# Attention and expert kernel: projections of local units an iteration earlier, parts stored once and repeated by the loads

## Chip, core and metric

One NeuronCore of a Trainium2 chip. The metric is the device time of one execution in microseconds (us); lower is better. Times come from repeated runs and from one profiled execution, whose trace has every instruction of the engines: PE (TensorE), DVE (VectorE), ACT (ScalarE), POOL (GpSimd) and SP (SyncE, which here only issues transfers).

## What is computed

Two layers on x of shape 8 x 512 x 128. Layer 1: attention with 16 heads of size 8 in which a query sees itself and 128 keys before it, an output projection, residual, layer norm. Layer 2: layer norm, causal attention with 16 heads, projection, residual, then a top-2 mixture of 8 experts (128 to 512 to 128, gelu), residual and layer norm. Cut to the attention:

```python
scores = jnp.einsum('bhtd,bhsd->bhts', q, k) * scale
scores = jnp.where(allowed, scores, -jnp.inf)   # j <= i, and j >= i - 128 in layer 1
attn = jax.nn.softmax(scores, axis=-1)
out = jnp.einsum('bhts,bhsd->bhtd', attn, v)
```

## The kernel before

**Units and iterations.** A unit is one batch element in one layer: units 0 to 7 are local (layer 1), 8 to 15 causal (layer 2). The iterations run from -2 to 16; iteration `it` does the scores, exponents, masks and values of unit `it`, the row maxima of unit `it + 1` (and the first of `it + 2`), and the tail (division, output projection, norms, routing) of unit `it - 1`. An iteration has 14 steps if its layer is local, 20 if causal (6 in iteration -2); in a step TensorE fills one pair of PSUM banks with scores, one or two with products for the maxima, and multiplies older probabilities by v. The PSUM pairs form a ring of three (L182 on) that scores, maxima, projections and turned outputs share. Every engine walks the same steps in its own program order; tables fix the order: `JOBS` (L166) gives side jobs their step, `project_at` (L174) the projection of q and k, `maxima_table` (L148) the maxima.

**Stacks.** To keep f32 accuracy with bf16 matmuls, q and k (after `project`, L1299) are split in three bf16 parts: HIGH by ACT (L740), the rest by DVE (L899), MIDDLE by ACT (L745), LOW by DVE (L905). A stack has 48 rows for each of two row groups (rows 0 to 47 and 64 to 111): six slots of 8 rows, and each slot holds one part of q or of k, so that one matmul over 48 rows sums the products of parts that matter. q has HIGH in slots 0 to 2, MIDDLE in 4 and 5, LOW in 3; k has HIGH in 2 to 4, MIDDLE in 1 and 5, LOW in 0. Two more rows hold the shift, the row maximum of each query (rows 48, 49). Three pairs of stacks exist; unit u uses pair u mod 3. The rows change partition on the way, so SP stores the parts to DRAM (`parts_dram`) and loads them back (`load_stacks`, L426 to L455): per unit six stores, in which each part is written once for every slot that it fills, and ten loads of 24, 16 or 8 rows of 8 KB. There is one copy of `parts_dram`, so a unit waits for the loads of the unit before.

**Order on SP's queue.** In iteration `it`: `load_stacks(it + 2)`, x_t of unit `it + 3` if that is local (L419), x_tok (L424), in causal iterations a slice of expert weights, and at last `load_shift(it + 1)` (L460), which waits for the shift of the next unit. SP's waits hold back all behind them.

**Other lines.** L1223/L1232 and L1252/L1258 are the products for the maxima, local and causal, L867 to L881 the maxima themselves, L889/L891 the splitting of the shift, L1341 its transpose, L784 its copy. L1198 are the scores, L707 their exponents, L603 to L619 the masks, L1278 the values. Of the tail: L913/L917 division, L1328/L1334 turned and projected outputs, L928/L935 residual sum, L941 to L945 `moments`, L954/L955 `variances`, L636/L638 `root` on POOL, L963/L974 `apply`, L1349/L768 the expert input xf, L1355/L985 logits, L777 `copy_rows`, L999 to L1009 `choose`, L1364 rank, L1020 to L1030 `place`, L628 `send`, an indirect store of 128 rows by POOL (eight per causal unit); `apply` of a unit waits until the sends of the unit before have landed. After the attention, 40 blocks of 256 rows run through the experts (L1415, L1434).

Of the kernel before, what the change touches and what calls it, by code (L numbers as in the profile page):

```python
# [70 lines left out]
STACK_LOADS = 5 * TILES_R * 16  # L71
# [76 lines left out]
def maxima_table():  # L148

    table = {}  # L150
    for u in range(UNITS):
        slots = []
        if u - 2 >= -1:
            n = steps(u - 2)
            slots += [(u - 2, k) for k in range(n - LEAD[layer(u - 2)], n)]
# [12 lines left out]
    CAUSAL: {0: ("xt",), 2: ("v",), 5: ("on",), 7: ("out",), 14: ("xf",), 15: ("shift",), 16: ("logits",), 18: ("rank",)},  # L168
# [5 lines left out]
def project_at(it, k):  # L174

    if it < 0:
        return k if it == -2 and 0 <= k < 2 else None
    return it + 2 if real(it + 2) and k == (0 if layer(it + 2) == LOCAL else 1) else None


def jobs_at(it, k):
# [6 lines left out]
    return out  # L188

# [26 lines left out]
def build(nc, x_t_in, x_in, w_in_all, pack_in, out):  # L216
    ctx = ExitStack()
    with ctx:
# [104 lines left out]
        scratch = nc.dram_tensor("parts_dram", (2, SLOTS, P, T), BF16, kind="Internal").ap()  # L323
# [23 lines left out]
        stored_high, stored_low = sem("stored_high"), sem("stored_low")  # L347
# [58 lines left out]
        def _(sp):  # L406
# [19 lines left out]
            def load_stacks(u):  # L426

                def store(part, ready):
                    sp.wait_ge(ready, u + 1)
                    for side, slots in ((0, Q_SLOTS), (1, K_SLOTS)):  # L430
                        place = scratch[side, slots[part]].rearrange("s p t -> p s t")
                        sp.dma_start(place, parts[:, part, side, :].unsqueeze(1).to_broadcast(place.shape)
                                     ).then_inc(stored_low if part else stored_high, 16)

                def load(side, first, last):
                    stack = (q_st, k_st)[side][u % STACKS]
                    by_row = scratch[side].rearrange("s (d r g) t -> (s d) r (g t)", d=HD, r=TILES_R)
                    for r in range(TILES_R):
                        sp.dma_start(stack[HALF * r + first:HALF * r + last, :, :].rearrange("p g t -> p (g t)"), by_row[first:last, r, :]  # L439
                                     ).then_inc(stack_in[u % STACKS], 16)  # L440

                if u:
                    sp.wait_ge(stack_in[(u - 1) % STACKS], ((u - 1) // STACKS + 1) * STACK_LOADS)
                store(0, high_ready)
                store(1, middle_ready)
                if u >= STACKS:
                    sp.wait_ge(score_filled, BEFORE[u - STACKS + 1])
                sp.wait_ge(stored_high, (u + 1) * 32)
                for side in range(2):
                    load(side, *HIGH_ROWS[side])  # L450
                store(2, low_ready)
                sp.wait_ge(stored_low, (u + 1) * 64)
                for side in range(2):
                    for rows_of_part in LOW_ROWS[side]:
                        load(side, *rows_of_part)  # L455
# [7 lines left out]
            for it in ITERATIONS:  # L463
# [3 lines left out]
                if it >= 0 and real(it + 2):  # L467
                    load_stacks(it + 2)
# [10 lines left out]
                if real(it + 1):  # L479
                    load_shift(it + 1)  # L480

# [52 lines left out]
        def _(pool):  # L534
# [49 lines left out]
            def plan_constants():  # L584

                pool.wait_ge(stored_high, UNITS * 32)
                pool.wait_ge(stored_low, UNITS * 64)
# [881 lines left out]
```

## Time and profile before

| | us |
|---|---|
| median of 3 runs (867.06 to 868.45) | 867.57 |
| profiled execution, its own time | 870.4 |
| span from its first to its last instruction | 868.6 |
| PE busy | 655.7 (75%) |
| DVE busy | 509.7 (59%) |
| ACT busy | 462.6 (53%) |
| POOL busy | 429.8 (49%) |

The profiled execution took 2.8 us more than the median of the runs; stretches and waits are read from it. The start takes it to 54.7 us, the local iterations to about 311, the causal ones to about 644, the expert blocks to 833, the last norm to the end. A row of a timeline is: start, duration, engine, line, instruction, shapes, count, and in brackets how long its engine was idle before it and what ended that. In the rows by windows the columns are named in the group's line.

### The profile page before, as it was taken

How to read it: one execution, taken by the hardware profiler on the slowest of the kernel's cores; microseconds unless marked ns; L12 is line 12 of the kernel's file. 1: busy time of each engine (PE TensorE's matmuls, PEld its weight loads, DVE VectorE, ACT ScalarE, POOL GpSimd, SP SyncE). 2: the span in 40 equal slices, each digit the busy share in tenths (PEclk: the TensorE clock that was granted, in tenths of full speed). 3: DMA queues.
4: the chain of work that ended last, by engine and by line, in shares of the span. 5: the costliest groups of instructions: out<-in, count | busy, mean ns of one | idle time of the engine just before them, and what ended most of it. 6: DMA issues, size and time to landing. Idle time of an engine off the chain costs nothing.

```text
span 868.6 us, 19900 instructions
## 1 busy us (share of the span) xinstructions
PE 655.7 (75%) x7512; PEld 393.1 (45%) x7512; DVE 509.7 (59%) x1116; ACT 462.6 (53%) x671; POOL 429.8 (49%) x649
## 2 busy tenths in 40 slices
PE   2557978978887878888788888886614999999900
PEld 0323434434443433444343444442313998898900
DVE  1644667676776888798888879882340222222236
ACT  2035655655674565766677666666502554554503
POOL 4015556556654543245464647458640454445445
PEclk8568999998997998999999999999855999999965
DMA  5635544643643637334362707101014566566464
GB/s 170 157 90 115 138 109 100 154 126 67 159 116 46 153 97 135 102 76 135 66 159 42 185 25 190 43 16 53 20 58 161 187 204 214 184 223 213 168 163 128
DMA packets 73583, 107.45 MB, mean 124 GB/s; under 512 B 8104, under 2 KB 60048, under 8 KB 70428
## 3 DMA queue, kind: packets, MB, share of 16 engines
q1 hardware_dynamic: 68892, 97.86, 42.2%
q0 software_dynamic: 4608, 8.47, 3.3%
q8 instruction: 54, 0.88, 0.5%
q14 instruction: 29, 0.24, 0.1%
HBM read 44.14 MB, written 38.90 MB: 96 GB/s over the span
## 4 chain that ended last, share of the span: by engine, by line
PE 32%; DMA 22%; DVE 17%; issue 10%; SPq 7%; POOL 6%; ACT 4%; another core or an unknown queue 0%; POOLq 0%; ACTq 0%; DVEq 0%
DMA parts_dram<-parts 9%; DMA arena<-parts_dram 7%; PE pair_ps L1415 6%; PE o_ps L1278 6%; SPq L439 4%; PE o_ps L1434 3%; PE pair_ps L1299 3%; PE pair_ps L1198 3%; POOL rows_dram L628 3%; DMA rows_dram<-rows,row_at 3%; PE misc L1434 3%; DVE row_max L878 2%; ACT probs L707 2%; DVE row_max L876 2%; PE pair_ps L1258 1%
## 5 line engine op out<-in xcount | busy, mean ns | idle before, releaser
L707 ACT ACTIVATE probs<-pair_ps 128x1024 f32<-128x1024 f32 x272 | 275.4, 1022 | 116.2 <-PE pair_ps L1198 107.5
L1278 PE MATMUL o_ps<-probs,v_aug 128*32 128x256 f32 (+3 forms) x2048 | 166.0, 421 | 9.1 <-POOL probs L616 3.5
L603 POOL TENSOR_SCALAR_AFFINE_SELECT probs<-probs 128x512 f32<-128x512 f32 x96 | 61.2, 637 | 140.4 <-ACT probs L707 139.4
L1198 PE MATMUL pair_ps<-arena 50*128 50x256 bf16 (+3 forms) x1024 | 108.2, 288 | 26.6 <-DMA arena<-shift_t 6.5
L673 POOL DMA_INDIRECT outputs_dram<-o_norm,arena x80 | 77.7, 971 | 100.5 <-DVE o_norm L1128 80.0
L867 DVE TENSOR_REDUCE row_max<-pair_ps 128x4 f32<-128x768 f32 x96 | 89.7, 953 | 46.7 <-PE pair_ps L1232 46.1
L838 ACT ACTIVATE probs<-pair_ps,arena 128x256 f32<-128x256 f32 x160 | 65.4, 471 | 76.3 <-PE pair_ps L1415 66.0
L876 DVE TENSOR_REDUCE row_max<-pair_ps 128x2 f32<-128x1024 f32 x64 | 77.2, 1219 | 15.8 <-PE pair_ps L1258 14.7
L1415 PE MATMUL pair_ps<-x_t,arena 128*128 128x256 f32 x320 | 80.8, 397 | 7.1 <-DMA arena<-pack 3.9
L1198 PEld LDWEIGHTS pair_ps<-arena 50*128 50x128 bf16 x1024 | 32.7, 95 | 108.9 <-issue 45.5
L1278 PEld LDWEIGHTS o_ps<-probs,v_aug 128*32 128x32 f32 x2048 | 48.6, 111 | 66.0 <-issue 39.5
L628 POOL DMA_INDIRECT rows_dram<-rows,row_at x64 | 63.4, 991 | 26.6 <-issue 15.7
L1223 PE MATMUL pair_ps<-window_b,ident_b 64*64 64x256 bf16 x384 | 32.1, 324 | 51.7 <-DMA arena<-parts_dram 43.1
L1415 PEld LDWEIGHTS pair_ps<-x_t,arena 128*128 128x128 f32 x320 | 59.8, 197 | 17.0 <-issue 8.9
L1252 PE MATMUL pair_ps<-first_b,eye_b 64*128 64x128 bf16 (+2 forms) x640 | 49.0, 232 | 22.7 <-ACT probs L707 8.7
L878 DVE TENSOR_REDUCE row_max<-pair_ps 128x2 f32<-128x768 f32 x64 | 60.9, 952 | 8.9 <-PE pair_ps L1258 8.9
L1124 DVE TENSOR_TENSOR o_norm<-o_ps,arena 128x256 f32<-128x256 f32 x20 | 8.5, 425 | 97.6 <-PE o_ps L1434 75.3
L1258 PE MATMUL pair_ps<-arena 48*128 48x384 bf16 (+3 forms) x512 | 62.4, 302 | 0.0
L605 POOL TENSOR_SCALAR_AFFINE_SELECT probs<-probs 128x512 f32<-128x512 f32 x96 | 60.9, 634 | 0.0
L611 POOL TENSOR_SCALAR_AFFINE_SELECT probs<-probs 128x256 f32<-128x256 f32 x64 | 26.0, 407 | 58.2 <-ACT probs L707 57.9
L899 DVE TENSOR_TENSOR rest<-pair_ps,parts 128x1024 f32<-128x1024 f32 x16 | 19.6, 1225 | 52.0 <-ACT parts L740 52.0
L1252 PEld LDWEIGHTS pair_ps<-first_b,eye_b 64*128 64x128 bf16 x640 | 26.3, 96 | 44.9 <-ACT probs L707 18.8
(147 smaller groups left out, 1107.8 us busy)
## 6 DMA issues: line engine op xcount, KB each, us to landing
arena<-pack SPq DMA_DIRECT2D x40, 578.0 KB
arena<-parts_dram SPq DMA_DIRECT2D x96, 192.0 KB
parts_dram<-parts SPq DMA_DIRECT2D x32, 384.0 KB
parts_dram<-parts SPq DMA_DIRECT2D x32, 256.0 KB
arena<-rows_dram SPq DMA_DIRECT2D x40, 130.0 KB
pack<-in_pack SPq DMA_DIRECT2D x8, 578.0 KB, 7.4
parts_dram<-parts SPq DMA_DIRECT2D x32, 128.0 KB
arena<-parts_dram SPq DMA_DIRECT2D x32, 128.0 KB
```

The costliest lines, as they stand in the source:

```text
L628: nc.gpsimd.indirect_dma_start(out=table[:, :], out_offset=bass.IndirectOffsetOnAxis(ap=row_at[:, j:j + 1], axis=0), in_=rows[:, j // NT, ...
L673: nc.gpsimd.indirect_dma_start(out=outputs[:, :], out_offset=bass.IndirectOffsetOnAxis(ap=place, axis=0), in_=block_y[i][:, t, :], in_offs ...
L707: nc.scalar.activation(probs[:, n % PROBS, :], pair_ps[RING_AT["score", n][0]][:, :, :].rearrange("p b t -> p (b t)"), ACT.Exp, scale=SCAL ...
L838: nc.scalar.activation(hidden[:, i * FT + f, :], hidden_ps[2 * i + f // 2][:, f % 2 * BLK:(f % 2 + 1) * BLK], ACT.Gelu_apprx_tanh, bias=bl ...
L867: nc.vector.tensor_reduce(top[:, i, :, 2 * g:2 * g + 2], pair[:, :, 0:2 * WIN].rearrange("p b (s k) -> p b s k", k=WIN), AX_X, ALU.max).th ...
L876: nc.vector.tensor_reduce(top[:, 3, :, 2 * g + m], pair[:, :, :], AX_X, ALU.max).then_inc(max_done, 1)
L878: nc.vector.tensor_reduce(top[:, 2, :, 2 * g + m - 2], pair[:, :, 0:3 * P], AX_X, ALU.max)
L1198: last = nc.tensor.matmul(pair[:, r, col:col + width], k_st[u % STACKS][own, gs, j * P:(j + 1) * P], q_st[u % STACKS][own, gs, q0:q0 + wid ...
L1252: nc.tensor.matmul(target[:, :, keys], eye_b[own, HALF * (1 - half):HALF * (1 - half) + P], first_b[r][own, half, keys].unsqueeze(1).to_br ...
L1258: last = nc.tensor.matmul(pair[:, r, col:col + keys], qs[own, gs, i * P:(i + 1) * P], ks[own, gs, 0:keys], start=False, stop=(n == len(wor ...
L1278: last = nc.tensor.matmul(o_ps[c * VHEAD:(c + 1) * VHEAD, q0:q0 + width], v_aug[u % 2][:, j, first:first + VHEAD], probs[:, slot, r * T + ...
L1415: last = nc.tensor.matmul(hidden_ps[2 * i + f // 2][:, f % 2 * BLK:(f % 2 + 1) * BLK], block_w[w][:, PACK_W1 + f * P:PACK_W1 + (f + 1) * P ...
```

## The change

- `project_at`: a local unit is projected three iterations ahead, at step 8, instead of two ahead at step 0. Causal units stay at step 1, two ahead. So unit 2 is projected in iteration -1, and iteration 5 has no projection.
- Each part is stored once (three stores per unit), into one of two copies of `parts_dram`; the loads repeat it, with a source whose outermost step is zero, into the slots (14 loads per unit). A unit waits for the stacks of the unit two before, not one. `load_stacks` of a local unit comes at the end of SP's iteration, after `load_shift`.
- `maxima_table`: the maxima of unit 1 all lie in iteration 0, so none stands before the first shift on PE.
- Causal side jobs: xf at step 13 (14), rank at 19 (18), moments 8 (9), variances 9 (10), apply 11 (12), copies of rows 13 (16), sends in steps 2 to 9 (0 to 7), `root` ahead of its step's mask, `top_two` ahead of its step's maxima. What follows a job of an iteration's last step is done in the next iteration's step 0. The moves of moments, variances and apply hold for local units too.

```diff
-Q_SLOTS = (slice(0, 3), slice(4, 6), slice(3, 4))
-K_SLOTS = (slice(2, 5), slice(1, 6, 4), slice(0, 1))
-HIGH_ROWS = ((0, 24), (16, 40))
-LOW_ROWS = (((24, 48),), ((0, 16), (40, 48)))
+LOW, MIDDLE, HIGH = 0, 1, 2
+Q_PARTS = {HIGH: ((0, HIGH, 3),), MIDDLE: ((4, MIDDLE, 2),), LOW: ((3, LOW, 1),)}
+K_PARTS = {HIGH: ((2, HIGH, 3),), MIDDLE: ((1, MIDDLE, 1), (5, MIDDLE, 1)), LOW: ((0, LOW, 1),)}
...
-STACK_LOADS = 5 * TILES_R * 16
+STACK_LOADS = 7 * TILES_R * 16
...
-        if u - 2 >= -1:
+        if u - 2 >= 0:
...
-    CAUSAL: {0: ("xt",), 2: ("v",), 5: ("on",), 7: ("out",), 14: ("xf",), 15: ("shift",), 16: ("logits",), 18: ("rank",)},
+    CAUSAL: {0: ("xt",), 2: ("v",), 5: ("on",), 7: ("out",), 13: ("xf",), 15: ("shift",), 16: ("logits",), 19: ("rank",)},
...
-    if it < 0:
-        return k if it == -2 and 0 <= k < 2 else None
-    return it + 2 if real(it + 2) and k == (0 if layer(it + 2) == LOCAL else 1) else None
+    if it == -2:
+        return k if 0 <= k < 2 else None
+    if k == 8 and real(it + 3) and layer(it + 3) == LOCAL:
+        return it + 3
+    return it + 2 if k == 1 and real(it + 2) and layer(it + 2) == CAUSAL else None
...
-        scratch = nc.dram_tensor("parts_dram", (2, SLOTS, P, T), BF16, kind="Internal").ap()
+        scratch = nc.dram_tensor("parts_dram", (2, PARTS, 2, P, T), BF16, kind="Internal").ap()
...
                 def store(part, ready):
                     sp.wait_ge(ready, u + 1)
-                    for side, slots in ((0, Q_SLOTS), (1, K_SLOTS)):
-                        place = scratch[side, slots[part]].rearrange("s p t -> p s t")
-                        sp.dma_start(place, parts[:, part, side, :].unsqueeze(1).to_broadcast(place.shape)
-                                     ).then_inc(stored_low if part else stored_high, 16)
+                    sp.dma_start(scratch[u % 2, part].rearrange("s p t -> p s t"), parts[:, part, :, :]).then_inc(stored[part], 16)
+
+                def load(part):
+                    sp.wait_ge(stored[part], (u + 1) * 16)
+                    for side, stack, pieces in ((0, q_st, Q_PARTS[part]), (1, k_st, K_PARTS[part])):
+                        source = scratch[u % 2, part, side].rearrange("(d r g) t -> d r (g t)", d=HD, r=TILES_R)
+                        for slot, _, times in pieces:
+                            for r in range(TILES_R):
+                                first = HALF * r + HD * slot
+                                place = stack[u % STACKS][first:first + HD * times, :, :].rearrange("p g t -> p (g t)")
+                                rows_of = source[:, r, :] if times == 1 else source[:, r, :].unsqueeze(0).to_broadcast([times, HD, GS * T])
+                                sp.dma_start(place, rows_of).then_inc(stack_in[u % STACKS], 16)
+
+                if u >= 2:
+                    sp.wait_ge(stack_in[(u - 2) % STACKS], ((u - 2) // STACKS + 1) * STACK_LOADS)
+                store(HIGH, high_ready)
+                store(MIDDLE, middle_ready)
                 if u >= STACKS:
                     sp.wait_ge(score_filled, BEFORE[u - STACKS + 1])
+                load(HIGH)
+                store(LOW, low_ready)
+                load(MIDDLE)
+                load(LOW)
...
-                if it >= 0 and real(it + 2):
+                if it >= 0 and real(it + 2) and layer(it + 2) == CAUSAL:
                     load_stacks(it + 2)
...
                     load_shift(it + 1)
+                if it >= -1 and real(it + 3) and layer(it + 3) == LOCAL:
+                    load_stacks(it + 3)
...
                 for k in range(steps(it)):
+                    if real(w) and k == 10:
+                        root(w)
                     if real(it):
                         mask(it, k)
-                    if real(w) and k == 10:
-                        root(w)
                     if real(w) and layer(w) == CAUSAL and k == 12:
                         add_residual(w)
-                    if real(it - 2) and layer(it - 2) == CAUSAL and k < CHOICES:
-                        send(it - 2 - B, k)
+                    if real(it - 2) and layer(it - 2) == CAUSAL and 2 <= k < 2 + CHOICES:
+                        send(it - 2 - B, k - 2)
```

## Rows read from the trace of the kernel before

**Rows 1.** The page: chain that ended last, by line, and local maxima (mean ns after busy us):
```profile
DMA parts_dram<-parts 9%; DMA arena<-parts_dram 7%; PE pair_ps L1415 6%; PE o_ps L1278 6%; SPq L439 4%; PE o_ps L1434 3%; PE pair_ps L1299 3%; PE pair_ps L1198 3%; POOL rows_dram L628 3%; DMA rows_dram<-rows,row_at 3%; PE misc L1434 3%; DVE row_max L878 2%; ACT probs L707 2%; DVE row_max L876 2%; PE pair_ps L1258 1%
...
L867 DVE TENSOR_REDUCE row_max<-pair_ps 128x4 f32<-128x768 f32 x96 | 89.7, 953 | 46.7 <-PE pair_ps L1232 46.1
```

**Rows 2.** The chain in order of time, the start: start, us, what:
```profile
9.43 3.71 DMA parts_dram<-parts
...
52.41 2.23 DMA arena<-shift_t
```

**Rows 3.** Timeline of PE: waits for stacks, and a projection at the slow clock:
```profile
28.71 0.43 PE L1223 MATMUL pair_ps<-window_b,ident_b 64*64 64x256 bf16 x4 [19.09 <-DMA arena<-parts_dram]
...
55.90 3.49 PE L1299 MATMUL pair_ps<-x_t,weights 128*128 128x512 f32 x4
...
80.83 0.43 PE L1223 MATMUL pair_ps<-window_b,ident_b 64*64 64x256 bf16 x4 [5.22 <-DMA arena<-parts_dram]
...
269.13 0.34 PE L1252 MATMUL pair_ps<-first_b,eye_b 64*128 64x128 bf16 x4 [4.18 <-DMA arena<-parts_dram]
...
306.14 0.26 PE L1252 MATMUL pair_ps<-first_b,eye_b 64*128 64x128 bf16 x4 [0.77 <-DMA arena<-parts_dram]
```

**Rows 4.** Windows (length; PE, PEld, DVE, ACT, POOL busy; clock, DMA share, GB/s), local iterations:
```profile
54.70:87.40 32.70, 25.39 (x369) 11.59 (x370) 16.75 (x18) 17.49 (x19) 16.19 (x26) 0.81 0.48 115
87.40:212.50 125.10, 105.57 (x1654) 53.77 (x1650) 86.73 (x149) 73.70 (x84) 73.82 (x109) 0.94 0.51 121
212.50:242.10 29.60, 24.72 (x416) 12.99 (x412) 20.62 (x34) 19.26 (x25) 18.67 (x28) 1.00 0.49 118
```

**Rows 5.** Windows with one kind of transfer: 24-row loads, shift, 128-partition weights, stores, 8-row loads:
```profile
132.00:133.00 1.00, 1.00 (x24) 0.47 (x24) 0.96 (x2) 0.62 (x1) 0.98 (x2) 1.00 0.84 197
147.10:147.50 0.40, 0.40 (x16) 0.16 (x8) 0.40 (x2) 0.40 (x1) 0.40 (x2) 1.00 0.12 36
654.50:658.00 3.50, 0.00 (x0) 0.00 (x0) 0.00 (x0) 0.00 (x0) 0.00 (x0) 0.50 0.84 339
126.00:128.00 2.00, 0.70 (x20) 0.22 (x12) 1.74 (x3) 2.00 (x4) 0.39 (x2) 1.00 1.03 346
24.30:26.90 2.60, 0.00 (x0) 0.00 (x0) 0.43 (x1) 0.00 (x0) 0.00 (x0) 0.50 0.51 85
```

**Rows 6.** Timeline of SP's queue: issues of stores and of stack loads:
```profile
13.15 1.55 SPq L439 DMA_DIRECT2D arena<-parts_dram  x4
...
252.19 1.74 SPq L439 DMA_DIRECT2D arena<-parts_dram  x4
```

**Rows 7.** Timelines of PE, ACT and DVE in iteration 2, S(2) = 118.96:
```profile
137.55 0.39 PE L1198 MATMUL pair_ps<-arena 50*128 50x256 bf16 x4
...
148.77 0.39 PE L1198 MATMUL pair_ps<-arena 50*128 50x256 bf16 x4 [0.98 <-DMA arena<-shift_t]
...
123.07 1.02 ACT L740 ACTIVATE parts<-pair_ps 128x1024 bf16<-128x1024 f32 x1 [2.65 <-PE pair_ps L1299]
...
126.47 1.23 DVE L905 TENSOR_TENSOR parts<-rest,parts 128x1024 bf16<-128x1024 f32 x1 [0.26 <-ACT parts L745]
...
143.67 0.24 DVE L891 SCALAR_TENSOR_TENSOR shift<-row_max,shift 128x64 bf16<-128x64 f32 x1
```

**Rows 8.** Timelines of DVE, ACT and PE in causal iterations 10 and 11:
```profile
434.45 0.16 DVE L1023 TENSOR_TENSOR next_row<-next_row,misc 128x8 f32<-128x8 f32 x1
...
461.12 1.37 DVE L974 TENSOR_SCALAR rows<-y,mean_var,rstd 128x128 f32<-128x128 f32 x4 [1.13 <-DMA rows_dram<-rows,row_at]
...
435.16 0.66 PE L1287 MATMUL misc<-ident,h_in 128*128 128x128 f32 x4
...
398.86 1.02 ACT L740 ACTIVATE parts<-pair_ps 128x1024 bf16<-128x1024 f32 x1 [1.43 <-PE pair_ps L1299]
...
392.94 0.39 PE L1198 MATMUL pair_ps<-arena 50*128 50x512 bf16 x2
...
423.58 0.25 PE L1252 MATMUL pair_ps<-first_b,eye_b 64*128 64x128 bf16 x4
```

More of the change, by code:

```diff
@@ L188, in jobs_at, with jobs_before @@
     return out
+def jobs_before(it, k):
+    if k:
+        return jobs_at(it, k - 1)
+    return jobs_at(it - 1, steps(it - 1) - 1) if it > -2 else []
 def turns_at(it, k):
@@ L346, in build @@
         middle_ready, low_ready = sem("middle_ready"), sem("low_ready")
-        stored_high, stored_low = sem("stored_high"), sem("stored_low")
+        stored = {part: sem(f"stored{part}") for part in (HIGH, MIDDLE, LOW)}
         stack_in = [sem(f"stack_in{i}") for i in range(STACKS)]
@@ L584, in plan_constants @@
             def plan_constants():
-                pool.wait_ge(stored_high, UNITS * 32)
-                pool.wait_ge(stored_low, UNITS * 64)
+                for part in (HIGH, MIDDLE, LOW):
+                    pool.wait_ge(stored[part], UNITS * 16)
                 nc.gpsimd.memset(not_after, 1.0).then_inc(plan_consts, 1)
@@ L737, in high_part @@
                 if u:
-                    act.wait_ge(stored_high, u * 32)
-                    act.wait_ge(stored_low, u * 64)
-                nc.scalar.activation(parts[:, 0, :, :], pair_ps[RING_AT["project", u][0]][:, :, :], ACT.Copy).then_inc(high_ready, 1)
+                    for part in (HIGH, MIDDLE, LOW):
+                        act.wait_ge(stored[part], u * 16)
+                nc.scalar.activation(parts[:, HIGH, :, :], pair_ps[RING_AT["project", u][0]][:, :, :], ACT.Copy).then_inc(high_ready, 1)
             def middle_part(u):
                 act.wait_ge(rest_ready, u + 1)
-                nc.scalar.activation(parts[:, 1, :, :], rest[:, :, :], ACT.Copy).then_inc(middle_ready, 1)
+                nc.scalar.activation(parts[:, MIDDLE, :, :], rest[:, :, :], ACT.Copy).then_inc(middle_ready, 1)
             def take_v(u):
@@ L798, in _ @@
                 for k in range(steps(it)):
-                    before = dict(jobs_at(it, k - 1))
+                    before = dict(jobs_before(it, k))
                     if "shift" in before:
@@ L898, in split_rest @@
                     dve.wait_ge(low_ready, u)
-                nc.vector.tensor_tensor(rest[:, :, :], pair_ps[RING_AT["project", u][0]][:, :, :], parts[:, 0, :, :], ALU.subtract
+                nc.vector.tensor_tensor(rest[:, :, :], pair_ps[RING_AT["project", u][0]][:, :, :], parts[:, HIGH, :, :], ALU.subtract
                                         ).then_inc(rest_ready, 1)
@@ L904, in low_part @@
                 dve.wait_ge(middle_ready, u + 1)
-                nc.vector.tensor_tensor(parts[:, 2, :, :], rest[:, :, :], parts[:, 1, :, :], ALU.subtract).then_inc(low_ready, 1)
+                nc.vector.tensor_tensor(parts[:, LOW, :, :], rest[:, :, :], parts[:, MIDDLE, :, :], ALU.subtract).then_inc(low_ready, 1)
             def divide(w):
@@ L1048, in _ @@
                 for k in range(steps(it)):
-                    before = dict(jobs_at(it, k - 1))
+                    before = dict(jobs_before(it, k))
+                    if "logits" in before:
+                        top_two(before["logits"])
                     if real(it + 1) and k == steps(it) - LEAD[layer(it)]:
@@ L1062, in _ @@
                     if real(w):
+                        if k == 8:
+                            moments(w)
                         if k == 9:
-                            moments(w)
-                        if k == 10:
                             variances(w)
-                        if k == 12:
+                        if k == 11:
                             apply(w)
-                    if "logits" in before:
-                        top_two(before["logits"])
                     if real(w) and layer(w) == CAUSAL and k == 17:
@@ L1111, in plan @@
                                                op0=ALU.mult, op1=ALU.add).then_inc(planned, 1)
+            place(UNITS - 1)
             plan()
```

20 lines of the change are left out of this document (1 added, 19 removed).

## The prediction

> **What bounds the kernel now.** I read the chain of waits first, then TensorE's own waits, then stretches of the timeline. The chain [rows 1] gives 16% of the span to storing the projected parts to DRAM and loading them back as stacks, more than to any matmul line. At the start that is nearly all there is: stores and loads of unit 0, one after the other, the same for unit 1, then the first shift [rows 2]. TensorE waits for stack 0 until 28.7 us, and then for one stack in each iteration, at step 11: 5.22 for stack 2, 4.18 for stack 8, 0.77 for stack 9 [rows 3]. So the local iterations are short of their loads, but by little: in a stretch of 29.6 to 32.7 us per iteration [rows 4] PE is busy 25, DVE 21, ACT 19. I call the start of iteration i's first scores S(i): S(0) 54.7, S(1) 87.4, S(5) 212.5, S(6) 242.1.
>
> **What the DMA rows say**, because the change rewrites the loads. The share of the 16 engines that a transfer keeps busy follows its leading count [rows 5]: the shift, 16 partitions into 2 rows, 0.12 (two of 16); the last loads of stack 0, 8 rows each, 0.51 (eight); a 24-row load 0.84 at 197 GB/s (twelve, and a bit of other traffic); transfers led by 128 partitions 0.84 to 1.03 at 339 to 346 GB/s. Where the two sides differ (16 and 2) the smaller decides. Four 24-row loads are issued within 1.55 us [rows 6] and don't spread over more engines, so they queue on the same ones. After the change the source of a repeated load has the repeat outermost: [3, 8 rows, 8 KB] against 24 rows, so its leading counts are 3 and 24. By the pattern of [rows 5] that is three engines, and for the MIDDLE q load (2 x 8) two. The rule that speaks against this change stands in the Trainium skill, DMA: Bandwidth & Descriptors, "Rules for kernel authors": a leading zero-stride broadcast of c copies confines a transfer to at most c engines. The trace agrees for the counts that it has (0.12, 0.51); it has no repeated load.
>
> **Price of a stack load.** The busiest engine gets 8 rows of each of four HIGH loads, 8 of each of two MIDDLE q loads, and one of each of eight 8-row loads: 56 rows of 8 KB, 459 KB. At 339 GB/s over 0.84 x 16 engines [rows 5] one engine moves 25.2 GB/s: 18.2 us (HIGH 10.4, MIDDLE 6.5, LOW 1.3). The LOW store (256 KB at 346 GB/s) queues among them: 0.76. Fixed cost 1.8: the shift takes 2.23 from issue to landing [rows 2], 0.45 of it moving 8 rows of 1 KB per engine at 18 GB/s. Together 20.8 us from first issue to landing. Bounds: three engines never beat twelve, so not below the 15.5 us of stack 0 today, 13.15 to 28.7 [rows 3, 6]; above, 16.4 GB/s per engine (197 over 12) gives 28 + 2.6 = 30.6. I take 25.2 since three engines share no row group, unlike twelve.
>
> **Start.** Removed: two thirds of each store's bytes, the wait of unit 1 for stack 0, and stack 1's place before the first shift. HIGH lands 3.71 - 512 KB/346 = 2.2 us after its issue instead of 3.71 [rows 2], so the first load goes at 11.8 instead of 13.15 [rows 6]. Stack 0 lands at 11.8 + 20.8 = 32.6 (28.7 today). The LOW store waits behind HIGH's rows until 24.8; only then may the scalar engine overwrite the parts for unit 1. Its HIGH store queues behind stack 0 and lands at 33.4, stack 1 at 54.2, and x_t for unit 2, issued after it on the same queue, at 54.9. The projection of unit 2, now in step 8 of iteration -1, needs that x_t; TensorE would be there at about 43. From 54.9: projection 3.49 at the slow clock [rows 3], high part 1.03, rest 1.23, a maximum 0.96, its wait 0.26, low part 1.23 [rows 7], two maxima 2.4, the split 0.5: 66.0. Shift transpose, copy, issue and landing 4.2: S(0) is 70.1 instead of 54.7. **+15.4.** If x_t weren't late, the 3.9 of stack 0 would be what is left; if it landed at the upper bound, +31.
>
> **Iteration 0.** No wait for stack 2 (5.22), no projection in step 0; three more of unit 1's maxima (3 x 0.953 on DVE [rows 1]). But the loads of unit 2 start after the first shift, x_t for unit 3 lands at S + 22.0, and TensorE reaches the projection at S + 17.3. Then 22.0 + 9.5 to the split + 4.3 = 35.8 for 32.7: **+3.1.**
>
> **Iterations 1 to 4.** The projection leaves step 0 (ACT waited 2.65 for it there [rows 7]) and the stack is in long before step 11. Without any DMA: step 8 began 18.6 after S(2) [rows 7]; 3.3 less for the projection and middle part, 1.3 for step 8 itself: TensorE is ready to project at S + 16.5. DVE then has sum, maximum, moments, rest, two maxima, low part and variances before the split, which ends at S + 25.3, where it ended at S + 24.9 before (143.91 - 118.96 [rows 7]). Shift landing follows in 4.1 to 4.9: 29.4, against 125.1/4 = 31.3 [rows 4]. Here the projection's x_t comes in again: stack loads are allowed from the last scores of the iteration before (2 us ahead of S), 20.8 - 0.9 later they leave the queue, x_t adds 0.75 and its receipt 0.9: S + 19.3. 2.8 late, so 32.2 per iteration, 128.8 for 125.1: **+3.7**. Cover for the loads of step 11 (S + 18.7 against S + 25) is ample.
>
> **Iteration 5** has no projection: 29.4 - 4.0 (1.23 + 1.23 + 1.5 idle) = 25.4 for 29.6 [rows 4]: **-4.2.**
>
> **Iterations 6 and 7** project causal units at step 1 as before. The first load of stack 8 goes 0.6 sooner than at 252.19 [rows 6], since the HIGH store is shorter; 20.8 later it is 272.4, where it was 269.1 [rows 3]: +3.2. The same count for stack 9 gives +3.3. **+6.5.**
>
> **Causal iterations.** (a) The placing of the rank moves behind the next iteration's first maximum: next_row was ready at 434.61 and the transpose of h went at 435.16 [rows 8]; now about 436.4, 1.1 net after the 1.0 that the rank no longer waits, in iterations 10 to 13: +4.4. (b) Stack: HIGH part at S + 5.9 (398.86 - 392.94 [rows 8]), the MIDDLE part and its store 3.8 later and (a), first load S + 10.8, 1.2 for the sends' packets, in at S + 32.8 against the need at S + 31.7 (423.58 - 392.94 [rows 8], plus (a)): about 0.9 x 5 = +4.5. Null rows queue behind unit 10's loads and the shift behind them: +1. (c) Moments, roots and apply a step earlier, sends two steps later: DVE already waits 1.13 for their landing [rows 8]; the sends meet fewer packets on 13 of 16 engines. Zero; bounds -2.2 (all such waits) and +5 per iteration. (d) Last iteration: sends start 0.7 later. xf, copies of rows and top_two move within their covers: nothing, 1 us each if DVE is late. **+10.6.** Expert blocks and the end: untouched.
>
> Sum 15.4 + 3.1 + 3.7 - 4.2 + 6.5 + 10.6 = 35.1, on the profiled execution's 870.4: 905.5; the median of the runs lies 2.8 under it: **903**.
>
> **Rivals.** **Loads keep their engines** (chance 0.15): if the descriptors are spread as today, S(0) comes 5.2 earlier, iteration 0 saves 4.4, 1 to 4 7.5, 5 4.2, 6 and 7 4.9, the causal part costs 1: -25, so 843. This is the side opposite to my forecast; for it speaks that stores and loads lead the chain [rows 1, 3]; against it that the pattern holds for 2, 8 and 24 rows [rows 5]. It decides from about 16 us per stack. **The narrow loads are hidden outside the start** (0.15): x_t lands within DVE's cover, only start and iterations 6, 7 pay: 15.4 + 6.5 + 1 - 4.2 - 7.5 = +11, 879. **The narrow engines run slower** (0.12): each microsecond more per stack costs about 2 at the start and one in some 12 later places; at 22 GB/s (+2.6) 939, at 16.4 GB/s over 1000. The forecast keeps 0.58.
>
> **Numbers.** Range 862 to 950: it leaves out the first rival and the worst of the third. About 0.2% is what a measurement of this kernel tells from no change. Faster 0.18 (first rival, part of the second), same 0.03, slower 0.79.
>
> **What would show it.** In windows with stack loads alone the DMA share falls to about 0.19 and 75 GB/s; TensorE waits for x_t at a projection (about 11 us in iteration -1, 2 to 3 in iterations 1 to 4); no wait for stacks at step 11 in local iterations; S(0) near 70. Wrong if the share stays near 0.8 during HIGH loads, or if S(0) comes before 54.7.

## The result and the profile after the change

**994.2 us** (median of 4 runs, 989.4 to 1001.3) against 868.0 for the kernel before (4 runs): ratio 1.146, 95% interval 1.138 to 1.154. I had predicted 903 with a range of 862 to 950. The sign was right and the size was not: I expected 35 us more and got 126. The profiled execution took 996.8, with a span of 995.0 against 868.6.

The page of the kernel after: span, busy time, DMA, memory traffic, and the chain that ended last by engine and by line.

```profile
span 995.0 us, 19930 instructions
...
PE 693.6 (70%) x7512; PEld 407.0 (41%) x7512; DVE 516.1 (52%) x1116; ACT 463.2 (47%) x671; POOL 430.4 (43%) x649
...
DMA packets 59887, 94.86 MB, mean 95 GB/s; under 512 B 6696, under 2 KB 46352, under 8 KB 56732
...
HBM read 44.14 MB, written 26.31 MB: 71 GB/s over the span
...
DMA 37%; PE 27%; SPq 10%; DVE 10%; issue 9%; ACT 4%; POOL 3%; another core or an unknown queue 1%; ACTq 0%; DVEq 0%; POOLq 0%
DMA parts_dram<-parts 21%; DMA arena<-parts_dram 7%; SPq L449 6%; DMA x_t<-in_x_t 6%; PE o_ps L1286 5%; PE pair_ps L1423 5%; PE pair_ps L1307 4%; PE o_ps L1442 2%; PE pair_ps L1206 2%; PE misc L1442 2%; PE pair_ps L1266 1%; DMA rows_dram<-rows,row_at 1%; DVE row_max L878 1%; ACT probs L714 1%; ACT parts L747 1%
```

The change kept its promise in bytes; the page of the kernel before has:

```profile
HBM read 44.14 MB, written 38.90 MB: 96 GB/s over the span
```

Yet the stores of the parts, 9% of the chain before [rows 1], are now 21%. Fewer bytes and a longer wait: that is a queue, not a volume. The windows say which queue. Two stretches in which stack loads are nearly all that moves (the LOW store or x_t, queued behind them, can have a small part; columns as in [rows 4]):

```profile
22.00:26.00 4.00, 0.00 (x0) 0.00 (x0) 0.00 (x0) 0.00 (x0) 0.00 (x0) 0.50 0.19 78
...
57.00:59.00 2.00, 0.00 (x0) 0.00 (x0) 0.00 (x0) 0.00 (x0) 0.00 (x0) 0.50 0.13 53
```

A share of 0.19 is three engines of sixteen, 0.13 is two; 78/3 and 53/2 are 26 GB/s for one engine. So the mechanism of the prediction is there: a source with the repeat outermost runs on as many engines as it makes copies, here three and two. The rule of the Trainium skill (DMA: Bandwidth & Descriptors, "Rules for kernel authors", at most c engines for a leading broadcast of c copies) agrees with both shares.

The chain in order of time, the start (start, us, what):

```profile
11.50 0.77 SPq L449
...
14.50 11.88 DMA parts_dram<-parts
...
35.75 0.72 SPq L449
...
38.70 12.83 DMA parts_dram<-parts
...
52.86 8.50 DMA x_t<-in_x_t
61.36 0.04 issue
61.41 3.79 PE pair_ps L1307 x4
```

The LOW store moves 256 KB. It takes 11.88 and 12.83 us here, and SP waits for it before it issues the last loads. Then x_t takes 8.50 us. I read both as packets that stand behind the rows of the stack loads on three engines; with these loads spread over eight engines (e1 below) the same store takes 9.06 and 6.90, and x_t 6.39. The same chain around S(1) = 117.67, in iteration 1, with x_t of unit 4 at its end:

```profile
114.65 0.66 SPq L465
...
116.11 4.02 DMA parts_dram<-parts
...
120.22 0.77 SPq L449
...
123.24 12.65 DMA parts_dram<-parts
...
137.22 8.34 DMA x_t<-in_x_t
145.56 0.04 issue
145.61 3.79 PE pair_ps L1307 x4
```

From the first stack load to x_t it is 25.3 us. TensorE's timeline shows what that makes of an iteration: L1206 at its start, L1307 the projection in step 8, with its wait for x_t in brackets.

```profile
77.00 0.60 PE L1206 MATMUL pair_ps<-arena 50*128 50x256 bf16 x4 [3.66 <-DMA arena<-shift_t]
...
102.27 3.78 PE L1307 MATMUL pair_ps<-x_t,weights 128*128 128x512 f32 x4 [10.33 <-DMA x_t<-in_x_t]
...
117.67 0.39 PE L1206 MATMUL pair_ps<-arena 50*128 50x256 bf16 x4 [1.04 <-DMA arena<-shift_t]
...
145.61 3.78 PE L1307 MATMUL pair_ps<-x_t,weights 128*128 128x512 f32 x4 [11.56 <-DMA x_t<-in_x_t]
...
161.57 0.61 PE L1206 MATMUL pair_ps<-arena 50*128 50x256 bf16 x4 [2.43 <-DVE row_max L874]
...
186.33 3.78 PE L1307 MATMUL pair_ps<-x_t,weights 128*128 128x512 f32 x4 [5.71 <-DMA x_t<-in_x_t]
...
202.26 0.61 PE L1206 MATMUL pair_ps<-arena 50*128 50x256 bf16 x4 [2.43 <-DVE row_max L874]
...
227.47 3.78 PE L1307 MATMUL pair_ps<-x_t,weights 128*128 128x512 f32 x4 [6.05 <-DMA x_t<-in_x_t]
...
243.40 0.61 PE L1206 MATMUL pair_ps<-arena 50*128 50x256 bf16 x4 [2.43 <-DVE row_max L874]
...
269.07 3.78 PE L1307 MATMUL pair_ps<-x_t,weights 128*128 128x512 f32 x4 [6.58 <-DMA x_t<-in_x_t]
```

Local iterations of 41 to 44 us where 31.3 was the mean of before [rows 4]. Note the 3.78: after each such wait the projection runs at the lower of the two clock levels; without the wait, in e5 below, it takes 1.98. The windows of two such projections, kernel after and e5, have a granted clock (third figure from the end) of 0.50 and 1.00:

```profile
186.50:190.00 3.50, 3.50 (x4) 1.00 (x4) 0.00 (x0) 0.00 (x0) 0.00 (x0) 0.50 0.00 0
```

```profile
105.70:107.60 1.90, 1.90 (x10) 0.66 (x8) 1.63 (x9) 0.12 (x1) 1.22 (x2) 1.00 0.21 43
```

The mean granted clock fell from 0.897 to 0.836, and the same 7512 matmuls keep PE busy 693.6 us instead of 655.7. Part of a wait's price is paid behind it.

In the causal part (425 to 710 us) three waits matter here (waited for: us in total, times, longest):

```profile
DVE rows L981 <- DMA rows_dram<-rows,row_at: 16.4, 5, 5.5
...
PE pair_ps L1260 <- DMA arena<-parts_dram: 16.1, 5, 4.6
...
PE misc L1295 <- DVE next_row L1030: 5.0, 4, 1.3
```

The second is the stacks again. The first has nothing to do with them: the vector engine waits for the sends of the unit before to land, before it may overwrite `rows`. The third is the placing of the rank, which now runs behind a maximum.

**Where the time went.** The SP timeline has the issue of every unit's first shift load; the differences between two of them, against before, cut the loss into stages. Every kernel of the experiments stands here too (us over the kernel before, each from its one profiled execution; the last column is the span's). One such column is good to some 5 us: two kernels with the same causal job order (e3 and c1) differ by 6 in the causal stage. The rows of n1, c2 and c3 flatter them: their profiled executions were their fastest, 11, 10 and 6 us under their medians; e3 and e5 were read at 4 under, b2 at 4 over.

| kernel | start | it. 0 | it. 1-4 | it. 5 | it. 6, 7 | units 8 to 15 | rest | span |
|---|---|---|---|---|---|---|---|---|
| forecast | +15.4 | +3.1 | +3.7 | -4.2 | +6.5 | +10.6 (with the rest) | | +35.1 |
| after | +22.2 | +8.8 | +40.7 | -0.1 | +10.6 | +41.7 | +2.5 | +126.4 |
| e1 split loads | +12.2 | +6.5 | +15.5 | -1.5 | +3.6 | +20.7 | -0.9 | +56.1 |
| e2 loads of before | +7.8 | +2.9 | +8.7 | -1.2 | +1.2 | +16.2 | +1.5 | +37.1 |
| e3 e2, early sends | +7.3 | +2.1 | +7.9 | -1.2 | +1.4 | -5.6 | 0.0 | +11.8 |
| e5 e2, x_t first | +1.4 | +0.5 | -1.9 | -5.4 | +3.0 | +14.1 | -2.0 | +9.8 |
| c1 e2, both | +1.7 | +0.7 | +3.6 | -4.3 | -2.4 | +0.4 | -0.8 | -1.0 |
| c3 c1, unit 2 late | -5.2 | +5.5 | -2.1 | -5.2 | -1.9 | +0.9 | +0.1 | -7.8 |
| n1 before, narrow loads | +10.6 | +7.9 | +24.8 | +7.3 | +12.1 | +36.2 | -3.9 | +95.0 |
| x1 after, x_t first | +14.5 | +3.8 | +27.2 | +2.7 | +8.9 | +41.3 | +0.9 | +99.4 |
| c4 after, both | +11.9 | +6.1 | +24.4 | +1.5 | +9.8 | +34.9 | -1.2 | +87.4 |
| b2 before, new side jobs | -0.1 | +0.4 | -2.3 | -0.2 | -1.5 | +17.3 | +4.3 | +17.9 |
| b1 before, early shift | -6.5 | -1.1 | -3.6 | +1.4 | -0.4 | -1.9 | +1.5 | -10.7 |
| c2 b1, jobs but not the sends | -6.1 | -1.5 | -6.7 | -1.7 | -1.9 | +0.5 | -1.4 | -18.7 |

### The profile page after: what moved, and what is told of

It reads as the page before. It is cut to its first block, busy times and chain, and to the rows that moved or that the text cites. A ratio compares the mean times of both kernels' runs of the same rounds, so it can differ in the third digit from the quotient of the medians.

```text
span 995.0 us, 19930 instructions
## 1 busy us (share of the span) xinstructions
PE 693.6 (70%) x7512; PEld 407.0 (41%) x7512; DVE 516.1 (52%) x1116; ACT 463.2 (47%) x671; POOL 430.4 (43%) x649
## 4 chain that ended last, share of the span: by engine, by line
DMA 37%; PE 27%; SPq 10%; DVE 10%; issue 9%; ACT 4%; POOL 3%; another core or an unknown queue 1%; ACTq 0%; DVEq 0%; POOLq 0%
DMA parts_dram<-parts 21%; DMA arena<-parts_dram 7%; SPq L449 6%; DMA x_t<-in_x_t 6%; PE o_ps L1286 5%; PE pair_ps L1423 5%; PE pair_ps L1307 4%; PE o_ps L1442 2%; PE pair_ps L1206 2%; PE misc L1442 2%; PE pair_ps L1266 1%; DMA rows_dram<-rows,row_at 1%; DVE row_max L878 1%; ACT probs L714 1%; ACT parts L747 1%
## 5 line engine op out<-in xcount | busy, mean ns | idle before, releaser
L1286 PE MATMUL o_ps<-probs,v_aug 128*32 128x256 f32 (+3 forms) x2048 | 177.5, 447 | 6.9 <-ACT o_t L722 3.0
L1206 PE MATMUL pair_ps<-arena 50*128 50x256 bf16 (+3 forms) x1024 | 115.2, 304 | 38.4 <-DVE rest L906 10.4
L1206 PEld LDWEIGHTS pair_ps<-arena 50*128 50x128 bf16 x1024 | 33.6, 97 | 129.4 <-issue 64.4
L1307 PE MATMUL pair_ps<-x_t,weights 128*128 128x512 f32 x64 | 43.8, 823 | 60.8 <-DMA x_t<-in_x_t 60.6
L1260 PE MATMUL pair_ps<-first_b,eye_b 64*128 64x128 bf16 (+2 forms) x640 | 51.9, 243 | 48.6 <-DMA arena<-parts_dram 30.7
L1286 PEld LDWEIGHTS o_ps<-probs,v_aug 128*32 128x32 f32 x2048 | 50.7, 116 | 71.3 <-issue 46.8
L747 ACT ACTIVATE parts<-pair_ps 128x1024 bf16<-128x1024 f32 x16 | 16.4, 1024 | 118.2 <-PE pair_ps L1307 102.7
L1266 PE MATMUL pair_ps<-arena 48*128 48x384 bf16 (+3 forms) x512 | 66.7, 319 | 0.0
```

The lines of the kernel that those rows point to most:

```text
L1206: last = nc.tensor.matmul(pair[:, r, col:col + width], k_st[u % STACKS][own, gs, j * P:(j + 1) * P], q_st[u % STACKS][own, gs, q0:q0 + wid ...
L1266: last = nc.tensor.matmul(pair[:, r, col:col + keys], qs[own, gs, i * P:(i + 1) * P], ks[own, gs, 0:keys], start=False, stop=(n == len(wor ...
L1286: last = nc.tensor.matmul(o_ps[c * VHEAD:(c + 1) * VHEAD, q0:q0 + width], v_aug[u % 2][:, j, first:first + VHEAD], probs[:, slot, r * T + ...
L1307: last = nc.tensor.matmul(pair[:, side, :], wq[layer(u)][:, side * C:(side + 1) * C], x_t[u % 2][:, :], start=True, stop=True)
```

## The experiments

The first four ask whether the narrow loads, the new order, or the repeated reading carry the loss.

**e1: split loads.** Every load has 8 rows and hence eight engines.

```diff
-rows_of = source[:, r, :] if times == 1 else source[:, r, :].unsqueeze(0).to_broadcast([times, HD, GS * T])
-sp.dma_start(place, rows_of).then_inc(stack_in[u % STACKS], 16)
+for copy in range(times):
+    first = HALF * r + HD * (slot + copy)
+    place = stack[u % STACKS][first:first + HD, :, :].rearrange("p g t -> p (g t)")
+    sp.dma_start(place, source[:, r, :]).then_inc(stack_in[u % STACKS], 16)
```

> The kernel after the change, with each repeated load replaced by as many loads of 8 rows as it made copies; stores, order and everything else stay. Theory 1 (few engines): the source with the repeat outermost holds a load to 3 or 2 engines, 0.31 us per 8 KB row, 24 us from the first load to the last landing. With 8 rows per load, 8 engines share 24 rows each: 7.4 us of moving at 0.31, up to 14.4 at 0.6, and 24 issues of 0.37 us, so a stack takes 12 to 16 us; the waits for x_t and for stacks go and the time falls to 840 to 865. Theory 2 (the new order is what costs: projection in step 8, side jobs moved): the time stays over 930. Theory 3 (reading the same DRAM rows three times is slow in itself): it stays near 990.

Measured 930.6 us (ratio to before 1.077, 1.070 to 1.083). That is 63.6 less than after, 66 more than my upper value for theory 1, and just at the edge of theory 2's "over 930": none of the three fits alone. The window of its HIGH loads, and a window of 24-row loads in e2 (stack 1; the LOW store issued at 32.57 may have a part in it):

```profile
18.00:22.00 4.00, 0.00 (x0) 0.00 (x0) 0.00 (x0) 0.00 (x0) 0.00 (x0) 0.50 0.55 80
```

```profile
32.00:34.00 2.00, 2.00 (x36) 1.68 (x38) 0.60 (x1) 0.60 (x1) 0.00 (x0) 0.50 0.74 198
```

Eight engines are busy and move 80 GB/s together, as much as three did. So engines alone are not what an 8-row load lacks; I had the row for it, 85 GB/s at 0.51 [rows 5], and read only the share. What the split gave back is the other traffic: from the first load of stack 1 to the projection that waits for x_t it is 32.63 to 51.36 here, 18.7 us, where after took 25.7 (35.75 to 61.41).

**e2: stores and loads of before in the new order.**

```diff
-sp.dma_start(scratch[u % 2, part].rearrange("s p t -> p s t"), parts[:, part, :, :]).then_inc(stored[part], 16)
+for side, slots in ((0, Q_SLOTS), (1, K_SLOTS)):
+    place = scratch[u % 2, side, slots[2 - part]].rearrange("s p t -> p s t")
+    sp.dma_start(place, parts[:, part, side, :].unsqueeze(1).to_broadcast(place.shape)).then_inc(stored[part], 16)
...
+by_row = scratch[u % 2, side].rearrange("s (d r g) t -> (s d) r (g t)", d=HD, r=TILES_R)
```

> The kernel after the change, with the stores and loads of before (each part stored once per slot, loads of 24, 16 and 8 rows from a source without a repeat), into two scratch copies so that the new order is kept. Theory 1 (few engines): a stack takes 15 to 16 us again as before the change, the stores cost 2 to 3 us more than in the kernel after: 840 to 865. Theory 2 (the new order costs): over 930. Theory 3 (repeated reads): 840 to 865, where the split loads stay near 990.

Measured 906.7 (1.047, 1.041 to 1.052). The new loads, with the stores that go with them, carry 87.5 us of the loss; but 39 remain that have nothing to do with them. Both ranges were missed: theory 1 had the larger part, theory 2 the rest. My rival "loads keep their engines" with its 843 is refuted as a forecast too, for the larger stores of this kernel, 2 to 3 us by my estimate, don't explain 64: the new order by itself makes the kernel slower.

**n1: the narrow loads in the old order** (e2 the other way round; the loads and stores of after in the kernel before).

```diff
-    load(side, *HIGH_ROWS[side])
...
+rows_of = source[:, r, :] if times == 1 else source[:, r, :].unsqueeze(0).to_broadcast([times, HD, GS * T])
```

> The kernel before the change, with only the stores and loads of after (one copy stored, the loads repeat it); its order of work is kept. Theory 1 (few engines): stack 0 lands near 35 instead of 28.7, stack 1 near 61; in a local iteration the loads start 10 us after the first scores and land 24 us later, some 8 us past the point where they are needed, in 6 to 7 iterations; the causal ones lose about as much: 960 to 1000 us. Theory 2 (the order costs): 865 to 890, since only the stores and loads differ.

Measured 976.0 (1.129, 1.124 to 1.135), as theory 1 said. Stack 0 is in at 34.8, and TensorE's waits for stacks at local maxima have doubled from 43.1 us to:

```profile
PE pair_ps L1218 <- DMA arena<-parts_dram: 88.5, 8, 25.0
```

**x1: x_t ahead of the stack loads.**

```diff
                     load_stacks(0)
+                    load_x_t(2)
                     load_stacks(1)
...
-                if real(it + 3) and it + 3 >= 2 and layer(it + 3) == LOCAL:
-                    load_x_t(it + 3)
...
+                if it >= -1 and real(it + 4) and layer(it + 4) == LOCAL:
+                    load_x_t(it + 4)
                 if it >= -1 and real(it + 3) and layer(it + 3) == LOCAL:
                     load_stacks(it + 3)
```

> The kernel after the change, with the load of x_t issued ahead of the stack loads instead of behind them (it must wait for the values of two units before, so the stack loads of an iteration start about 4 us later); nothing else. Theory 1: the 60.6 us that TensorE waits for x_t in 7 waits go, but the stack itself then lands some 28 us after the first scores against a need at 25: local iterations of 34 to 36 instead of 41, and the start 5 us shorter: 955 to 970. Rival (the total of DMA work is the limit, whatever its order): 985 to 1000.

Measured 970.9 (1.122, 1.115 to 1.128), a fraction over the range. The waits for x_t are gone but for the 4.1 of the first projection of all, which the kernel before has too (60.6 us in 7 in the kernel after), and the stacks are late instead, as the lines of its waits show; in the kernel after the first of them was 28.9 in 2:

```profile
PE pair_ps L1232 <- DMA arena<-parts_dram: 44.7, 7, 25.1
...
PE pair_ps L1261 <- DMA arena<-parts_dram: 23.5, 5, 9.3
```

So more than half of the x_t wait only covered the stack's: 56.5 us of it bought 23. The next four split the 39 us of the new order.

**e3: e2 with the sends and the rank where they were.**

```diff
-... 16: ("logits",), 19: ("rank",)},
+... 16: ("logits",), 18: ("rank",)},
-                    if real(it - 2) and layer(it - 2) == CAUSAL and 2 <= k < 2 + CHOICES:
-                        send(it - 2 - B, k - 2)
+                    if real(it - 2) and layer(it - 2) == CAUSAL and k < CHOICES:
+                        send(it - 2 - B, k)
```

> The kernel of e2 (new order, loads of before), with the rank back in step 18 and the sends back in steps 0 to 7 of a causal iteration; moments, roots, apply and the copies of rows stay a step or more earlier. Theory 1 (late sends): in e2 the vector engine waits for the landing of the sends 16.7 us in 5 waits before it may write the next rows (before: 2.2 in 3); sends two steps earlier take that away, and the placing no longer runs behind a maximum: 16 to 21 us less than the 906.7 of e2, so 886 to 891. Rival (the wait only hides one that TensorE or the stacks would show anyway): 902 to 908.

Measured 885.7 (1.024, 1.017 to 1.031): 21 us less, the lower end of theory 1's range. Two changes are in it, the sends and the rank; no run has one without the other, only the waits part them. The waits for the sends over the five causal iterations in which they occur, in before (386 to 584 us), e2 (400 to 620) and e3 (395 to 600):

```profile
DVE rows L974 <- DMA rows_dram<-rows,row_at: 2.2, 3, 1.1
```

```profile
DVE rows L989 <- DMA rows_dram<-rows,row_at: 16.7, 5, 4.9
```

```profile
DVE rows L989 <- DMA rows_dram<-rows,row_at: 5.9, 3, 2.3
```

By these waits the sends account for 10.8 of the 21. The rank has about 5 of them: in the same window of e2 TensorE waits for its placing, a wait that before and e3 do not have. Some 5 us stay without a name.

```profile
PE misc L1303 <- DVE next_row L1038: 5.2, 4, 1.3
```

The timeline of e2 shows the mechanism of the sends in two lines: the last of eight sends is issued in step 9, and the write of the next rows, moved up to step 11, waits for its landing.

```profile
522.65 0.98 POOL L643 DMA_INDIRECT rows_dram<-rows,row_at  x1 [0.17 <-issue]
```

```profile
529.15 1.12 DVE L989 TENSOR_SCALAR rows<-y,mean_var,rstd 128x128 f32<-128x128 f32 x4 [4.38 <-DMA rows_dram<-rows,row_at]
```

**b2: the new side jobs alone, in the kernel before** (rank 19, sends from step 2, moments, roots and apply a step earlier, copies of rows in step 13).

```diff
-CAUSAL: {..., 14: ("xf",), 15: ("shift",), 16: ("logits",), 18: ("rank",)},
+CAUSAL: {..., 13: ("xf",), 15: ("shift",), 16: ("logits",), 19: ("rank",)},
...
-    send(it - 2 - B, k)
+    send(it - 2 - B, k - 2)
...
-    if k == 12:
+    if k == 11:
         apply(w)
```

> The kernel before the change, with only the side jobs reordered as in the change (rank in step 19, sends from step 2, moments, roots and apply a step earlier, copies of rows in step 13). Theory 1 (late sends): some 4 us in each of 5 causal iterations: 885 to 892. Rival (a loss only together with the new stack loads, whose packets the sends meet): 866 to 874.

Measured 883.8 (1.018, 1.012 to 1.024), just under theory 1's range; +17.3 stands in the causal stage, and the other stages add up to 0.6. It takes no narrow load to produce this loss. (c2 below keeps everything of this but the moved sends and rank, and the loss is gone.)

**e5: e2 with x_t ahead of the stack loads** (the edit of x1).

> The kernel of e2, with the load of x_t ahead of the stack loads. In e2 TensorE waits 19.5 us in 4 waits for x_t at the projection (7.5 in iteration -1, 3.8 in iteration 0, 3.4 in iteration 1). If these waits are on the path, 10 to 15 us go and the time is 892 to 897; if the stack loads, now some 4 us later, or the vector engine take their place, 902 to 908.

Measured 884.5 (1.021, 1.015 to 1.027): 22 us less, more than I expected and more than the waits for x_t themselves (19.5). The projection, no longer behind a wait, runs at the higher clock:

```profile
105.66 1.98 PE L1316 MATMUL pair_ps<-x_t,weights 128*128 128x512 f32 x4
```

**b1: only the first shift moved up, in the kernel before.**

```diff
-        if u - 2 >= -1:
+        if u - 2 >= 0:
...
-scratch = nc.dram_tensor("parts_dram", (2, SLOTS, P, T), BF16, kind="Internal").ap()
+scratch = nc.dram_tensor("parts_dram", (2, 2, SLOTS, P, T), BF16, kind="Internal").ap()
...
-                if u:
-                    sp.wait_ge(stack_in[(u - 1) % STACKS], ((u - 1) // STACKS + 1) * STACK_LOADS)
+                if u >= 2:
+                    sp.wait_ge(stack_in[(u - 2) % STACKS], ((u - 2) // STACKS + 1) * STACK_LOADS)
```

> The kernel before the change, with two scratch copies (unit 1's store no longer waits for the loads of stack 0) and all of unit 1's maxima in iteration 0, so that the first shift doesn't wait for stack 1; nothing else. If stack 1 was what held the first shift, S(0) comes 4 to 7 us sooner than 54.7 and iteration 0 gets 3 us longer: 862 to 867. If TensorE's slow clock and the maxima of unit 0 hold it anyway: 868 to 872.

Measured 859.1 (0.990, 0.985 to 0.995), 3 us under my range: **1% faster than the kernel before**, a small gain but clear of the interval. S(0) comes at 48.20 instead of 54.69:

```profile
48.20 0.61 PE L1198 MATMUL pair_ps<-arena 50*128 50x256 bf16 x4 [3.60 <-DMA arena<-shift_t]
```

The last four put the parts together: c1 = e3 + e5, c4 the same with the narrow loads, c3 and c2 two ways to do better.

> e3 and e5 in one: the new order with the loads of before, x_t ahead of the stack loads, rank in step 18 and sends from step 0. If the two losses add up (21 and 22 us of the 906.7 of e2), 861 to 866. If they share a wait, 870 to 880.

Measured 867.8 (1.000, 0.996 to 1.004), between my two ranges. The losses nearly add up, 39 of 43 us. With them gone, the new order as a whole neither gains nor loses against before. That is not yet the early projection: c1 also holds b1's gain. It is c2 (last below) with the projection moved to step 8 and, to serve it, the stack loads and x_t at the end of SP's iteration, and it is 6.6 us slower than c2 (867.8 against 861.2, 12 runs each). So on fast loads the early projection costs some 7 us, which is what the first shift gains.

> The kernel after the change with its narrow loads, x_t ahead of the stack loads, rank in step 18 and sends from step 0. If the price of the narrow loads doesn't depend on the order, this lies as far over c1 as the kernel after lies over e2 (87 us): 945 to 955. If the repaired order gave the narrow loads room to hide in, it would be under 930.

Measured 959.2 (1.107, 1.100 to 1.113), 4 us over the range and 91.4 over c1 (87.5 between after and e2): the price of the narrow loads hardly depends on the order's two faults. In the old order it is higher, 108 (n1, 976). So with narrow loads the repaired order is worth 17 us; how much of that is the early projection and how much b1's first shift, no run parts.

```diff
+    if it == 0 and k == 0:
+        return 2
-    if k == 8 and real(it + 3) and layer(it + 3) == LOCAL:
+    if it >= 0 and k == 8 and real(it + 3) and layer(it + 3) == LOCAL:
```

> c1 with the projection of unit 2 back in step 0 of iteration 0, so that the first shift waits neither for x_t of unit 2 nor for that projection; units 3 to 7 are projected an iteration ahead as in c1. S(0) then comes near 48 as in b1 instead of near 56, and iteration 0, which now has two projections, gets 4 to 6 us longer: 2 to 4 us less than c1, 858 to 863. If the second projection waits for parts that are still being stored, no gain or a loss of 2 to 5.

Measured 868.9 (1.004, 1.000 to 1.007), a miss: the start is 7 us shorter than in c1, but iteration 0 with its two projections gives back 4.8, and the medians don't differ clearly (868.9 against 867.8).

c2 takes b1, and from b2 all but the moved rank and sends:

> b1 (before, first shift moved up, two scratch copies) with the harmless part of the reordered side jobs: moments, roots and apply a step earlier, xf and copies of rows in step 13, the top two a step's start earlier, but rank in step 18 and sends from step 0. If only the sends and the placing cost something in b2 (883.8 against 866.6), this is within 3 us of b1's 859; if the earlier apply meets the sends too, it is 3 to 8 us slower than b1.

Measured 861.2 (0.995, 0.991 to 0.998), within 3 us of b1. So the earlier moments, roots and apply cost nothing clear by themselves. (Its profiled execution, the -18.7 of the table, was the fastest of its twelve, 851.7.)

## Why the prediction was wrong

**Right: direction, mechanism, places.** Engines follow the leading count: forecast 0.19 and 75 GB/s, measured 0.19 and 78. TensorE waits for x_t at every early projection, only longer: 16.2 us in iteration -1 (forecast 11), 5.7 to 11.6 in iterations 1 to 4 (forecast 2 to 3). The chain of the start came in the forecast order, each event later: stack 0 at 35.1 (forecast 32.6), x_t of unit 2 at 61.4 (54.9), S(0) at 77.0 (70.1).

The miss of 91 us by stages (after against forecast): start 6.8, iteration 0 5.7, iterations 1 to 4 37, iteration 5 4.1, iterations 6 and 7 4.1, causal part with the rest 33.6.

**Step 1 that failed, "Price of a stack load", 20.8 us, up to x_t 21.5.** Measured 25.7 in the start and 25.3 in iteration 1. The rate of a narrow engine by itself was right (26 against 25.2 GB/s). One candidate for the missing 4 us: not all 56 rows of the busiest engine run at it. 8 of them belong to 8-row loads, which keep eight engines busy at once, and [rows 5] had 85 GB/s over eight, 10.6 for each. Eight rows at 10.6 GB/s are 6.2 us instead of the 2.6 in my sum, so 24.4 in all and 25.1 up to x_t. This estimate was made afterwards and meets the total, but not its parts. In iteration 1 the LOW store lands 15.7 us after the first load is issued (120.22 to 135.88), where my sum had 13.0; so 2.7 of the missing 3.8 us lie ahead of this landing, while half of the 8-row loads, those of LOW, are issued only after it and the other half right behind the store. Two windows show the ends of the stretch:

```profile
120.20:123.20 3.00, 2.45 (x43) 1.63 (x40) 1.53 (x2) 1.97 (x4) 1.61 (x4) 1.00 0.11 26
...
141.00:145.00 4.00, 0.00 (x0) 0.00 (x0) 0.00 (x0) 0.00 (x0) 0.00 (x0) 0.50 0.13 50
```

In the first 3 us, while SP issues the four HIGH loads (2.97 us, where my rows had 1.55), little moves; at the end two engines move 25 GB/s each, as I had reckoned. So the term was 4 us too small; whether the slow start, the 8-row loads or the stores among them took these is open.

**Step 2, "stack loads are allowed from ... 2 us ahead of S".** They are allowed, but the HIGH store isn't issued before the shift, which stands ahead of it in SP's queue. It lands 4.0 us later, so the first load goes at S + 2.5 (120.22 against 117.67). In iteration 1 steps 1 and 2 together give 27.9 from S to the projection where I had 19.3; in iterations 2 to 4 it is 24.8, 25.2 and 25.7. That is 6.6 late on average; 1.8 more for a projection at 3.78 instead of 1.98; 8.4 of the 9.2 us that each of these iterations missed my number by. Four times this is 37 of the 91 us of the whole miss.

**Step 3, causal (c), "Zero; bounds -2.2 and +5 per iteration".** It was 2.8 per iteration by the waits (16.4 us in 5 against 2.2 in 3), 14 in all. The argument (fewer packets in the way) looked at the path of one send and not at the eight that are issued one after the other: sends two steps later and their reader a step earlier close a gap of three steps, and there was a wait of 1.13 already [rows 8], no gap. e3 gets 21 us back, b2 produces 17; in both the rank moves with the sends. The rank's own term, (a) with its 4.4, was right: the wait for its placing is 5.0 us in 4.

**Step 4, causal (b), 0.9 per iteration.** With loads of 25 rather than 21 us it was 2.2 to 4.6 at L1260, 16.1 us in 5 waits; iterations 6 and 7 lost 10.6 for 6.5, and iteration 5 lost its gain of 4.2, 3.2 of it in a wait for a stack, which I had excluded:

```profile
307.99 0.43 PE L1231 MATMUL pair_ps<-window_b,ident_b 64*64 64x256 bf16 x4 [3.19 <-DMA arena<-parts_dram]
```

The waits of (a), (b) and (c) come to 35 of the 44 us of the causal part; the other 9 are not traced.

**The rival that came.** "The narrow engines run slower, each microsecond more per stack costs about 2 at the start and one in some 12 later places" had the right shape for the wrong reason: in the clean windows a narrow engine moved 25 to 26 GB/s, and the whole load was longer all the same. The slope can now be estimated: e1 shortens first load to projection by 7.0 us and gains 63.6, e2 by 9.7 (to 16.0, 30.99 to 46.95) and gains 87.5. That is 9 us of time for each microsecond per stack in both, less than my 14, presumably because some of the later places have slack. The forecast's 903 leaned on the lower part of the range from 15.5 to 30.6 that I had written down for this one term; at a slope of 9, that range alone makes 855 to 991.

**The order of work.** In my sum the schedule was worth 25 us ("loads keep their engines", 843). In truth (e2) it cost 39: x_t put behind the stacks 22, the sends with the rank 21, and the rest comes to zero (c1) only because the first shift gains what the early projection costs, some 7 us each (b1, and c1 against c2). The early projection moves a wait rather than removing it: ACT waits 25.8 us for projections in c1 and 29.7 in c2, DVE 48.0 and 50.8 for the HIGH parts that follow. And unit 2's projection now stands ahead of the first shift: c1's start is 7.8 us longer than c2's.

**Left open.** The 24 us between e1 and e2: 8-row against 24-row loads, 24 against 10 DMAs per stack, and the same DRAM rows read three times differ together. The 80 to 85 GB/s of an 8-row load also stand in the kernel before, which reads nothing twice, so the form could be enough as a cause, but no run separates it. Open, too, is where in a stack load the missing 4 us arise (step 1).

## What to carry to other kernels

Count engines before bytes: a load that repeats its source is cheap in bytes, but if the repeat is outermost it runs on as many engines as copies (three and two here), and what was issued behind it, the small store (11.2 to 12.8 us) and the next input (8.3 to 9.0), came late with it. Issue the small input that someone waits for ahead of the big loads. When producer and consumer of one buffer are both moved, add both moves before you call the slack unchanged; and try the parts of a change alone, since here one part (the first shift moved up, with the second scratch copy it needs) was a gain of 1%, buried under the losses of the others.

## What was not expected of the hardware

- Eight engines on 8-row loads move 80 GB/s at a share of 0.55, three engines on loads of 3 x 8 rows 78 at 0.19, twelve on 24-row loads 198 at 0.74. The busy share says how many engines are held, not what they move.
- Issuing a load with a repeated source costs SP more. Four of them, of the same size, took 2.95 us (0.74 each), where four plain 24-row loads take 1.55 [rows 6]:

```profile
11.50 2.95 SPq L449 DMA_DIRECT2D arena<-parts_dram  x4
```

- TensorE ran the projection in 3.78 us behind each of its waits of 5.7 to 16.2 us for x_t, at the lower of its two clock levels (granted clock 0.50), and in 1.98 (clock 1.00) in iterations 0 to 4 of e5, where the wait was gone.
